# Two-layer cross-attention kernel: the context accumulated with its features on partitions

## The chip, the cores and the metric

The kernel runs on one core of a Trainium2 chip. The metric is the device time of one execution in microseconds (us), lower is better. Everything is one launch: a program for TensorE (PE in the profile), VectorE (DVE), ScalarE (ACT), GpSimd (POOL) and SyncE (SP), which keep step by semaphores alone.

## The reference

x and ctx are 8 sequences of 128 tokens with 128 features. Two layers follow each other, each an attention and a feed-forward part (FFN), all with residuals:

```python
x = x + xattn0(layernorm(x), ctx, ctx, mask, ...)   # 16 heads of 8, relative position bias, mask
x = x + ffn0(layernorm(x))                          # low rank: gelu((x U1) V1 + b1) U2 V2 + b2
x = x + xattn1(layernorm(x), ctx, ctx, ...)         # 16 heads of 8, no bias, no mask
x = x + moe(layernorm(x))                           # 16 experts of width 64, best 8, one shared expert
```

Either attention computes per head, with V = ctx Wv + bv:

```python
attn = softmax(energy)                # 128 queries x 128 keys
x = einsum('bhqk,bhkd->bhqd', attn, V)
x = concat(heads) @ Wo + bo
```

The softmax's division is put behind the product with V: the kernel multiplies unnormalized weights with V and with ones, and divides the one by the other. The part from there to `@ Wo` is called the context here.

## The kernel before

The 8 sequences are taken in 4 pairs (PAIRS); the two sequences of a pair are the batches b = 0, 1. A pass i of the loop body does layer 0 of pair i and, interleaved by hand, layer 1 of pair i - 1. The first pass (i = 0) has no layer 1, the last one (i = 3) doesn't start a new pair, and a tail behind it does layer 1 of the last pair. In the trace the first pass lies at about 27 to 69 us, the second to 130, the third to 191, the last to 252, the tail to 297. Each engine's order is written out in its own `body`, and an engine never goes past an instruction that waits.

PSUM has 8 banks of 128 x 512 fp32, in three rings: "m" (banks 4 to 6) for single results, "s" (0 and 1) for scores, "t" (2 and 3) for turned weights. BODY (L81) names the uses of a ring in order, and use n takes bank n modulo the ring's length: `fill` (L121) lets TensorE wait until the earlier use of that bank is freed, `filled` announces the result, `read` waits for it, `free` hangs on the reader's last instruction and gives the bank back, and `freed` waits for that. Of the "m" ring the text needs these. In the first pass the order is C00, xcT, C01, k0, k1, q0, o0 (L102), so k0 gets the bank of C00, q0 that of C01, and o0 that of k0. In the later passes it has C10, C11, o1, C00, C01, xn3T, logit, o0, so logit gets the bank of C00 and o0 that of C01.

The context of layer l and batch b:

- `values` (L1075, TensorE): the weights `pt` (keys on partitions, 128 queries per head slot) come in four chunks c of four slots s, each copied from PSUM by ScalarE. The stationary operand of a head is `va`, 128 keys x 32 columns (VW): 8 value features, a column of ones, and zeros. A matmul of slot s writes 32 partitions, at 32 j, and 128 columns of C, at 128 g; head = 8 (s % 2) + s // 2, j = head // 4, g = head % 4. So 16 matmuls fill a bank, with queries on columns. fp32 matmuls show as two records each.
- `context` (L758, VectorE): per batch a transpose of 32 x 32 blocks from PSUM to `ct1`, which frees the bank; the reciprocal of the row sums (`crc`, 16 columns); the multiply into `ct2`; and a second block transpose to `ct3`, features on partitions. Every kind is done for both batches before the next kind.
- `attention_out` (L1089, TensorE): waits for both `ct3` and multiplies with `wo` into o0 or o1. `add_residual` (L779), the variance, POOL's power (L375) and `normalize` (L721) follow.

TensorE's order around it: in the first pass values(0, 0), later values(0, 1), then keys(0) and keys(1) (L1015) and queries(0) (L1020) of the next pair, then attention_out(0). In the later passes values(1, 0), the turned scores of batch 1 (L1071), values(1, 1), half of the turned weights of layer 0 (L1060), attention_out(1), the other half, values(0, 0), values(0, 1), turn_tokens(3) (L999), logits (L1121), attention_out(0). The FFN of layer 0 has its matmuls at L1102 and L1113; L878 is VectorE's last addition before the output.

POOL does `add_value_bias` (L400; the operation is L406) once per layer and pair, one addition that writes the 8 value columns of all heads of both batches of `va`. In its order it stands, for layer 1, ahead of power(3) (the variance behind add_residual(1)). The splits of the next keys and queries (L394, L383, L398, L387) stand ahead of power(1) in the first pass. At the start VectorE clears `va` and sets its column of ones (L900, L902).

Of the kernel before, what the change touches and what calls it, by code (L numbers as in the profile page):

```python
# [11 lines left out]
ALU = mybir.AluOpType  # L12
AX = mybir.AxisListType

BATCH, SEQ, D = 8, 128, 128
# [23 lines left out]
VW = 32  # L39


def bass_xattn_ffn_moe(nc, x_d, ctx_d, mask_d, wqk_d, wv_d, wo_d, bqk_d, bv_d, rows_d, table_d, u1t_d, v1_d, b1_d,
# [3 lines left out]
    with ExitStack() as ctx:  # L46
# [166 lines left out]
        pt = sb("pt", [128, 2, 2, HEADS, SEQ])  # L213
        ct1 = sb("ct1", [128, 2, 4, 4, 32])
        crc = sb("crc", [128, 2, 4, 4])
        ct2 = sb("ct2", [128, 2, 4, 4, DK])
        ct3 = sb("ct3", [128, 2, 2, SEQ])
# [153 lines left out]
        def _(pool):  # L371
# [28 lines left out]
            def add_value_bias(l, p, turn):  # L400
                if l == 0:

                    freed(pool, "m", "v1", turn)
                elif not (isinstance(turn, int) and turn == 0):
                    read(pool, "m", "C11", turn)
                pool.tensor_tensor(va[:, l, :, :, 0:DK],  # L406
                                   vf[:].rearrange("p (b l h d) -> p b l h d", b=2, l=2, d=DK)[:, :, l],
                                   bvb[:].rearrange("p b (l h d) -> p b l h d", l=2, d=DK)[:, :, l],
                                   ALU.add).then_inc(sem(f"va{l}"), 1)

# [294 lines left out]
        def _(dve):  # L705
# [52 lines left out]
            def context(l, p, turn):  # L758

                for b in range(2):  # L760
                    src = read(dve, "m", f"C{l}{b}", turn)
                    free(dve.transpose(ct1[:, b], src[:]), "m", f"C{l}{b}", turn)  # L762
                for b in range(2):
                    freed(dve, "m", f"C{l}{b}", turn)
                    dve.reciprocal(crc[:, b], ct1[:, b, :, :, DK]).then_inc(sem(f"crc{l}"), 1)
                for b in range(2):
                    after(dve, f"crc{l}", p, b + 1, 2)
                    dve.tensor_tensor(ct2[:, b].rearrange("p q g d -> p g q d"), ct1[:, b, :, :, 0:DK],
                                      crc[:, b].unsqueeze(3).broadcast_to([128, 4, 4, DK]), ALU.mult)\
                       .then_inc(sem(f"ct2{l}"), 1)  # L770
                for b in range(2):
                    after(dve, f"ct2{l}", p, b + 1, 2)
                    dve.transpose(ct3[:, l, b], ct2[:, b]).then_inc(sem(f"ct3{l}"), 1)

# [125 lines left out]
            dve.memset(va[:], 0.0).then_inc(sem("va_zeros"), 1)  # L900
            dve.wait_ge(sem("va_zeros"), 1)
            dve.memset(va[:, :, :, :, DK:DK + 1], 1.0).then_inc(sem("va_cleared"), 1)  # L902
            dve.wait_ge(sem("ident_in"), 16)
# [89 lines left out]
        def _(pe):  # L993
# [81 lines left out]
            def values(l, b, p, turn):  # L1075

                if b == 0:
                    after(pe, f"va{l}", p)
                dst = fill(pe, "m", f"C{l}{b}", turn)
                for c in range(4):  # L1080
                    freed(pe, "t", f"T{l}{b}{c}", turn)
                    for s in range(4 * c, 4 * c + 4):
                        head = HALF * (s % 2) + s // 2
                        j, g = head // 4, head % 4
                        ins = pe.matmul(dst[32 * j:32 * j + VW, g * SEQ:(g + 1) * SEQ], va[:, l, b, head],  # L1085
                                        pt[:, l, b, s], start=True, stop=True)
                filled(ins, "m", f"C{l}{b}", turn)

            def attention_out(l, p, turn):  # L1089
                after(pe, f"ct3{l}", p, of=2)  # L1090
                dst = fill(pe, "m", f"o{l}", turn)
# [288 lines left out]
```

## Time and profile before

| | |
|---|---|
| time, median of 3 runs | 300.1 us (300.08, 300.1, 301.48) |
| span of the profiled execution | 296.9 us (its own full time is not given) |
| PE busy | 209.6 us, 71% |
| PE weight loads | 154.6 us, 52% |
| DVE busy | 198.1 us, 67% |
| ACT busy | 118.0 us, 40% |
| POOL busy | 83.7 us, 28% |
| chain that ended last, by engine | PE 33%, DVE 27%, issue 15%, POOL 7%, ACT 6%, DMA 5%, SP's queue 5% |

Busy times overlap between engines and say only how full each is. The chain follows back from the last instruction to what released each step; its shares tell where the end is set. Times in the rows are in us from the start of the span unless marked ns.

### The profile page before, as it was taken

What the parts mean: (1) busy time and instruction counts of PE and PEld (TensorE: products, weight loads), DVE (VectorE), ACT (ScalarE), POOL (GpSimd) and SP (SyncE); (2) the same over time, 40 slices, a digit from 0 to 9 for tenths busy, and PEclk for the clock granted to TensorE, in tenths of its full rate; (3) what the DMA queues carried; (4) which work ended last, traced back from release to release, by engine and by line L of the source; (5) the groups of instructions that cost most, each with busy time, mean ns of one, the idle gap of its engine ahead of it and who ended that gap; (6) DMA issues with size and microseconds to landing.
All of it is one profiled execution on the core that took longest, in us unless ns stands there. A gap on an engine that the chain in (4) does not pass through costs nothing.

```text
span 296.9 us, 4777 instructions
## 1 busy us (share of the span) xinstructions
PE 209.6 (71%) x1541; PEld 154.6 (52%) x1541; DVE 198.1 (67%) x561; ACT 118.0 (40%) x273; POOL 83.7 (28%) x110
## 2 busy tenths in 40 slices
PE   2723674555987868767887787777976979572996
PEld 1422553343655747535566565554765756251684
DVE  4656866246886786678876976678578764915673
ACT  2500664603587363305683452153552612061221
POOL 1402676134436131315281312150412011000000
PEclk9955699555599999995899999967799889779699
DMA  3553612102101220030002200200020002000000
GB/s 110 185 144 99 235 46 67 49 2 59 33 3 25 62 64 13 11 97 0 2 15 58 70 18 0 67 5 4 7 51 0 0 2 53 20 2 2 0 0 18
DMA packets 21895, 12.61 MB, mean 42 GB/s; under 512 B 2966, under 2 KB 20998, under 8 KB 21878
## 3 DMA queue, kind: packets, MB, share of 16 engines
q1 hardware_dynamic: 20790, 11.88, 14.7%
q10 hardware_dynamic: 1088, 0.52, 0.7%
q8 instruction: 9, 0.15, 0.2%
q14 instruction: 8, 0.07, 0.1%
HBM read 5.44 MB, written 0.54 MB: 20 GB/s over the span
## 4 chain that ended last, share of the span: by engine, by line
PE 33%; DVE 27%; issue 15%; POOL 7%; ACT 6%; DMA 5%; SPq 5%; DVEq 0%; POOLq 0%; ACTq 0%
PE bank L1130 5%; PE bank L1085 4%; PE bank L1150 4%; DVE mx L743 3%; DVE xn L721 3%; POOL rstd L375 3%; ACT pt L554 3%; PE bank L1071 3%; POOL es L416 2%; DVE ct L762 2%; SPq L258 2%; SPq L261 2%; PE bank L1102 2%; DVE es L733 2%; PE bank L1039 2%
## 5 line engine op out<-in xcount | busy, mean ns | idle before, releaser
L416 POOL TENSOR_TENSOR es<-es,mx 128x512 f32<-128x512 f32 x32 | 33.4, 1055 | 37.9 <-DVE mx L728 36.8
L542 ACT ACTIVATE es<-es 128x512 f32<-128x512 f32 x32 | 19.1, 625 | 33.9 <-POOL es L416 33.8
L1060 PE MATMUL bank<-ident,es 128*128 128x128 f32 x128 | 25.4, 346 | 9.9 <-ACT es L542 9.7
L375 POOL TENSOR_TENSOR rstd<-ve,half 128x2 f32<-128x2 f32 x16 | 11.2, 699 | 73.8 <-DVE ve L715 73.4
L593 ACT ACTIVATE gth<-bank 128x256 f32<-128x256 f32 (+1 forms) x36 | 13.2, 380 | 34.1 <-PE bank L1130 34.0
L733 DVE TENSOR_TENSOR es<-bank,biasq 128x512 f32<-128x512 f32 x32 | 21.2, 684 | 7.8 <-PE bank L1044 7.7
L1060 PEld LDWEIGHTS bank<-ident,es 128*128 128x128 f32 x128 | 19.0, 178 | 14.1 <-ACT es L542 13.7
L1130 PE MATMUL bank<-xnT,wg 128*128 128x256 f32 (+1 forms) x72 | 25.6, 439 | 0.6 <-DVE gb L858 0.4
L852 DVE SCALAR_TENSOR_TENSOR ga<-gth,bank 128x256 f32<-128x256 f32 (+1 forms) x36 | 15.0, 416 | 15.0 <-ACT gth L593 14.9
L1085 PE MATMUL bank<-pt,va 128*32 128x128 f32 x512 | 24.8, 290 | 0.0
L1130 PE MATMUL bank<-xnT,wu 128*128 128x256 f32 (+1 forms) x72 | 22.9, 403 | 0.0
L1150 PE MATMUL bank<-wd,hT 128*128 128x128 f32 x128 | 20.9, 287 | 2.9 <-DVE hT L872 2.8
L547 ACT ACTIVATE pt<-bank 128x512 f32<-128x512 f32 x32 | 18.3, 593 | 11.7 <-PE bank L1060 11.5
L743 DVE TENSOR_REDUCE mx<-bank 128x4 f32<-128x512 f32 x32 | 20.3, 684 | 3.5 <-PE bank L1039 3.2
L554 ACT ACTIVATE pt<-bank 128x512 f32<-128x512 f32 x32 | 17.4, 594 | 11.8 <-PE bank L1071 11.6
L762 DVE STREAM_TRANSPOSE ct<-bank 128x512 f32<-128x512 f32 x16 | 11.0, 705 | 16.3 <-PE bank L1085 16.2
L1085 PEld LDWEIGHTS bank<-pt,va 128*32 128x32 f32 x512 | 20.7, 116 | 2.2 <-issue 1.1
L1150 PEld LDWEIGHTS bank<-wd,hT 128*128 128x128 f32 x128 | 18.1, 193 | 6.6 <-DVE hT L872 5.3
L728 DVE TENSOR_REDUCE mx<-es 128x4 f32<-128x512 f32 x32 | 21.0, 676 | 0.0
L999 PE MATMUL bank<-ident,xn 128*128 128x128 f32 x24 | 6.0, 337 | 20.2 <-DVE xn L721 20.2
L721 DVE TENSOR_SCALAR xn<-x,mv,rstd 128x128 f32<-128x128 f32 x32 | 12.9, 444 | 9.6 <-POOL rstd L375 9.6
L1044 PE MATMUL bank<-kst,qst 96*128 96x128 bf16 x128 | 13.6, 254 | 6.2 <-DVE es L733 3.6
(132 smaller groups left out, 408.8 us busy)
## 6 DMA issues: line engine op xcount, KB each, us to landing
kst<-ksp SPq DMA_DIRECT2D x24, 64.0 KB, 2.6
qst<-qsp SPq DMA_DIRECT2D x48, 32.0 KB
kst<-ksp SPq DMA_DIRECT2D x48, 32.0 KB
qst<-qsp SPq DMA_DIRECT2D x24, 64.0 KB, 2.5
biasq<-rel_bias_scratch SPq DMA_DIRECT2D x2, 512.0 KB, 4.6
wg<-in_wg SPq DMA_DIRECT2D x1, 544.0 KB, 4.1
wu<-in_wu SPq DMA_DIRECT2D x1, 544.0 KB, 5.6
wd<-in_wd SPq DMA_DIRECT2D x1, 512.0 KB, 5.7
```

What stands on the lines that cost most here:

```text
L375: pool.tensor_tensor(rstd[:, n, :], ve[:, n, :], half[:, 0:2], ALU.pow).then_inc(sem(f"rstd{n}"), 1)
L416: pool.tensor_tensor(es[:, b, h], es[:, b, h], mx[:, 0, b, h].unsqueeze(2).broadcast_to([128, 4, SEQ]), ALU.subtract).then_inc(sem(f"less0 ...
L542: act.activation(es[:, b, h], es[:, b, h], ACT.Exp, scale=-1.0).then_inc(sem(f"p0{b}"), 1)
L554: free(act.activation(pt[:, 1, b, 4 * c:4 * c + 4, :], src[:], ACT.Exp), "t", f"T1{b}{c}", turn)
L721: dve.tensor_scalar(xn[n][:, b], src[:, b], mv[:, n, b, 0:1], rstd[:, n, b:b + 1], ALU.subtract, ALU.mult).then_inc(sem(f"xn{n}"), 1)
L728: dve.tensor_reduce(mx[:, 0, b, 4 * c:4 * c + 4], es[:, b, 4 * c:4 * c + 4], AX.X, ALU.min)\
L733: free(dve.tensor_tensor(es[:, b, 4 * c:4 * c + 4], src[:].rearrange("p (h k) -> p h k", h=4), biasq[:, 2 * c:2 * c + 2].rearrange("p a b ...
L743: free(dve.tensor_reduce(mx[:, 1, b, 4 * c:4 * c + 4], src[:].rearrange("p (h k) -> p h k", h=4), AX.X, ALU.max), "s", f"S1{b}{c}", turn)
L1060: ins = pe.transpose(dst[:, s * SEQ:(s + 1) * SEQ], es[:, b, 4 * c + s], ident[:])
L1085: ins = pe.matmul(dst[32 * j:32 * j + VW, g * SEQ:(g + 1) * SEQ], va[:, l, b, head], pt[:, l, b, s], start=True, stop=True)
L1130: ins = pe.matmul(dst[0:rows, k * TOK:(k + 1) * TOK], w[:, c * 128:c * 128 + rows], xnT[3][:], start=True, stop=True)
L1150: ins = pe.matmul(Y_BANK[:, b * D:(b + 1) * D], hT[0:rows, c % 2, b * SEQ:(b + 1) * SEQ], wd[:, c] if c < ECH else swd[:], start=(c == 0 a ...
```

## The change

`values` now uses a different place for each head. In chunk c the four slots go to the four strips of 32 partitions, and the four chunks accumulate in the same 128 columns: `va` holds a head's 8 value columns at column 8 c of its 32, the others are zero. A second set of four matmuls per chunk, with the stationary operand `vones` (ones in the 8 columns at 8 c), accumulates the row sums in the next 128 columns, so that each sum stands on the same 8 partitions as the features that it divides. 32 matmuls per bank in place of 16, and C comes out with features on partitions.

`context` has four operations in place of eight: per batch a reciprocal of 128 x 128 from PSUM, then per batch a multiply from PSUM into `ct3`, which now frees the bank. `attention_out` waits for the freed banks. POOL adds the value bias in four pieces. The rows of `wo` and the columns of `wv` and `bv` are put in another order on the host.

The diff, cut (the same reordering of `bv` is left out):

```diff
@@ -211,9 +211,8 @@
         pt = sb("pt", [128, 2, 2, HEADS, SEQ])
-        ct1 = sb("ct1", [128, 2, 4, 4, 32])
-        crc = sb("crc", [128, 2, 4, 4])
-        ct2 = sb("ct2", [128, 2, 4, 4, DK])
+        vones = sb("vones", [128, 4, VW])
+        crc = sb("crc", [128, 2, SEQ])
         ct3 = sb("ct3", [128, 2, 2, SEQ])
@@ -403,10 +402,12 @@
-                pool.tensor_tensor(va[:, l, :, :, 0:DK],
-                                   vf[:].rearrange("p (b l h d) -> p b l h d", b=2, l=2, d=DK)[:, :, l],
-                                   bvb[:].rearrange("p b (l h d) -> p b l h d", l=2, d=DK)[:, :, l],
-                                   ALU.add).then_inc(sem(f"va{l}"), 1)
+                for c in range(4):
+                    h = slice(4 * c, 4 * c + 4)
+                    ins = pool.tensor_tensor(va[:, l, :, h, DK * c:DK * c + DK],
+                                             vf[:].rearrange("p (b l h d) -> p b l h d", b=2, l=2, d=DK)[:, :, l, h],
+                                             bvb[:].rearrange("p b (l h d) -> p b l h d", l=2, d=DK)[:, :, l, h], ALU.add)
+                ins.then_inc(sem(f"va{l}"), 1)
@@ -759,18 +760,11 @@
                 for b in range(2):
                     src = read(dve, "m", f"C{l}{b}", turn)
-                    free(dve.transpose(ct1[:, b], src[:]), "m", f"C{l}{b}", turn)
-                for b in range(2):
-                    freed(dve, "m", f"C{l}{b}", turn)
-                    dve.reciprocal(crc[:, b], ct1[:, b, :, :, DK]).then_inc(sem(f"crc{l}"), 1)
-                for b in range(2):
+                    dve.reciprocal(crc[:, b], src[:, SEQ:2 * SEQ]).then_inc(sem(f"crc{l}"), 1)
+                for b in range(2):
+                    src = read(dve, "m", f"C{l}{b}", turn)
                     after(dve, f"crc{l}", p, b + 1, 2)
-                    dve.tensor_tensor(ct2[:, b].rearrange("p q g d -> p g q d"), ct1[:, b, :, :, 0:DK],
-                                      crc[:, b].unsqueeze(3).broadcast_to([128, 4, 4, DK]), ALU.mult)\
-                       .then_inc(sem(f"ct2{l}"), 1)
-                for b in range(2):
-                    after(dve, f"ct2{l}", p, b + 1, 2)
-                    dve.transpose(ct3[:, l, b], ct2[:, b]).then_inc(sem(f"ct3{l}"), 1)
+                    free(dve.tensor_tensor(ct3[:, l, b], src[:, 0:SEQ], crc[:, b], ALU.mult), "m", f"C{l}{b}", turn)
@@ -898,8 +892,11 @@
             dve.memset(va[:], 0.0).then_inc(sem("va_zeros"), 1)
-            dve.wait_ge(sem("va_zeros"), 1)
-            dve.memset(va[:, :, :, :, DK:DK + 1], 1.0).then_inc(sem("va_cleared"), 1)
+            dve.memset(vones[:], 0.0).then_inc(sem("va_zeros"), 1)
+            dve.wait_ge(sem("va_zeros"), 2)
+            for c in range(4):
+                ins = dve.memset(vones[:, c, DK * c:DK * c + DK], 1.0)
+            ins.then_inc(sem("va_cleared"), 1)
@@ -1079,15 +1076,17 @@
                 for c in range(4):
                     freed(pe, "t", f"T{l}{b}{c}", turn)
-                    for s in range(4 * c, 4 * c + 4):
-                        head = HALF * (s % 2) + s // 2
-                        j, g = head // 4, head % 4
-                        ins = pe.matmul(dst[32 * j:32 * j + VW, g * SEQ:(g + 1) * SEQ], va[:, l, b, head],
-                                        pt[:, l, b, s], start=True, stop=True)
+                    for s in range(4):
+                        pe.matmul(dst[VW * s:VW * s + VW, 0:SEQ], va[:, l, b, 4 * c + s], pt[:, l, b, 4 * c + s],
+                                  start=(c == 0), stop=(c == 3), skip_group_check=True)
+                    for s in range(4):
+                        ins = pe.matmul(dst[VW * s:VW * s + VW, SEQ:2 * SEQ], vones[:, c], pt[:, l, b, 4 * c + s],
+                                        start=False, stop=(c == 3), skip_group_check=True)
                 filled(ins, "m", f"C{l}{b}", turn)
...
             def attention_out(l, p, turn):
-                after(pe, f"ct3{l}", p, of=2)
+                for b in range(2):
+                    freed(pe, "m", f"C{l}{b}", turn)
...
+    by_slot = lambda w: w.reshape(w.shape[0], 2, HALF, DK).swapaxes(1, 2).reshape(w.shape)
+    by_row = lambda w: by_slot(w.T).T.reshape(4, 4, DK, D).swapaxes(0, 1).reshape(D, D)
...
-        "wv": _np.stack([a["L0_xattn_Wv"], wv1], 1),
-        "wo": _np.stack([a["L0_xattn_Wo"], a["L1_xattn_Wo"]], 1),
+        "wv": _np.stack([by_slot(a["L0_xattn_Wv"]), by_slot(wv1)], 1),
+        "wo": _np.stack([by_row(a["L0_xattn_Wo"]), by_row(a["L1_xattn_Wo"])], 1),
```

## Rows read from the trace of the kernel before

**Rows 1.** Chain of waits, start and first pass: start us, us, what

```profile
24.34 2.30 DMA qst<-qsp
...
43.44 1.50 PE bank L1085 x32
...
46.85 0.70 PE bank L1093 x4
...
49.62 0.71 POOL rstd L375
```

**Rows 2.** Chain of waits, third pass

```profile
152.64 1.50 PE bank L1085 x32
...
156.51 0.72 PE bank L1093 x4
...
162.53 0.73 PE bank L1093 x4
```

**Rows 3.** Chain of waits, last pass and tail

```profile
208.68 2.72 PE bank L1085 x32
...
266.56 1.50 PE bank L1085 x32
...
269.93 0.73 PE bank L1093 x4
```

**Rows 4.** Page, costliest groups: busy us, mean ns, idle before

```profile
L1085 PE MATMUL bank<-pt,va 128*32 128x128 f32 x512 | 24.8, 290 | 0.0
```

**Rows 5.** Two instants, L1085 on PE: slice, length, busy (records in flight), clock, DMA

```profile
37.30:37.31 0.01, 0.01 (x6) 1.00 0.00 0
...
37.64:37.65 0.01, 0.01 (x11) 1.00 0.00 0
```

**Rows 6.** Timeline, third pass, PE: start, us, instruction, idle before and releaser

```profile
158.02 2.49 PE L1085 MATMUL bank<-pt,va 128*32 128x128 f32 x64
...
160.44 0.44 PE L999 MATMUL bank<-ident,xn 128*128 128x128 f32 x2
...
161.35 0.62 PE L1121 MATMUL bank<-gateT,xnT 128*128 128x16 f32 x4 [0.47 <-ACT xnT L489]
```

**Rows 7.** Instructions of the tile ct on DVE: ns min/median/max, first and last start

```profile
L762 DVE STREAM_TRANSPOSE ct<-bank x16: 672/708/718, 41.1 to 268.1; 128x512 f32<-128x512 f32 x16
L765 DVE RECIPROCAL crc<-ct x16: 207/220/234, 45.6 to 268.9; 128x16 f32<-128x16 f32 x16
L768 DVE TENSOR_TENSOR ct<-ct,crc x16: 253/280/698, 45.9 to 269.2; 128x128 f32<-128x128 f32 x16
L773 DVE STREAM_TRANSPOSE ct<-ct x16: 261/284/305, 46.3 to 269.6; 128x128 f32<-128x128 f32 x16
```

**Rows 8.** The smallest reciprocal, and a 128-column operation out of PSUM, same columns

```profile
L831 DVE RECIPROCAL swr<-sws x4: 166/166/166, 106.7 to 277.8; 128x2 f32<-128x2 f32 x4
...
L878 DVE TENSOR_TENSOR xout<-bank,x x8: 281/286/292, 130.1 to 294.3; 128x128 f32<-128x128 f32 x8
```

**Rows 9.** Timeline, first pass, PE and POOL

```profile
44.84 1.13 PE L1015 MATMUL bank<-xcT_sb,wqk 128*128 128x256 f32 x4
...
45.82 0.67 PE L1020 MATMUL bank<-xcT_sb,wqk 128*128 128x256 f32 x2
...
48.84 0.67 POOL L387 TENSOR_TENSOR qsp<-qr,qsp 128x256 bf16<-128x256 f32 x1
```

**Rows 10.** Instructions of L406 on POOL: ns min/median/max, first and last start

```profile
L406 POOL TENSOR_TENSOR va<-vf,bvb x8: 713/728/1167, 23.5 to 215.1; 128x256 f32<-128x256 f32 x8
```

**Rows 11.** Chain, first pass's FFN, and timeline of the same matmuls in the third

```profile
52.99 3.80 PE bank L1102 x8
...
60.25 3.77 PE bank L1113 x16
...
68.56 1.23 PE bank L1020 x2
...
176.90 1.95 PE L1113 MATMUL bank<-w,fh 128*128 128x128 f32 x16
```

More of the change, by code:

```diff
@@ L1352 @@
                           _np.stack([by_dim(wq1), by_dim(wk1)], 1)], 1),
-        "wv": _np.stack([a["L0_xattn_Wv"], wv1], 1),
-        "wo": _np.stack([a["L0_xattn_Wo"], a["L1_xattn_Wo"]], 1),
+        "wv": _np.stack([by_slot(a["L0_xattn_Wv"]), by_slot(wv1)], 1),
+        "wo": _np.stack([by_row(a["L0_xattn_Wo"]), by_row(a["L1_xattn_Wo"])], 1),
         "bqk": _np.stack([by_dim(a[f"L{l}_xattn_b{c}"].reshape(D)) for l in range(2) for c in "qk"], 1),
-        "bv": _np.tile(_np.concatenate([a["L0_xattn_bv"], a["L1_xattn_bv"].reshape(D)]), (2, 1)),
+        "bv": _np.tile(_np.concatenate([by_slot(a["L0_xattn_bv"].reshape(1, D))[0],
+                                        by_slot(a["L1_xattn_bv"].reshape(1, D))[0]]), (2, 1)),
         "rows": _np.stack([_np.tile(a[n], (2, 1)) for n in ("L0_xattn_bo", "L0_ffn_b2", "L1_xattn_bo")]),
```

## The prediction

> **What bounds the kernel now.** I read the page first: no engine is busy all the time, so the end is set by a chain, and the chain of waits has to be read stretch by stretch. At the places that the diff touches it always has the same order: the value matmuls of the second batch, VectorE's context work, the output projection. In the first pass these are the rows at 43.44 (ends 44.94) and 46.85, and the POOL step at 49.62 follows from them [rows 1]. In the third pass they are 152.64 (ends 154.14) and 156.51 for layer 1, and layer 0's projection follows at 162.53 [rows 2]; the second pass has the same distances. The last pass has a value stage at half clock, and the tail has one more layer-1 stage [rows 3]. So there are eight contexts, layer 0 in four passes, layer 1 in three and the tail, and all eight are on the chain.
>
> **Part 1, TensorE: 16 more matmuls per batch.** One value stage is 16 fp32 matmuls, two records each, in 1.50 us [rows 1]; it becomes 64 records. It matters in which column strips they lie. Now the matmuls alternate between two strips (head 0 in strip 0, head 8 in strip 2) and after eight of them go to the other two. A record lasts 0.29 us on average [rows 4]. One instant inside such a stretch has 6 records in flight; one at the change-over, when four strips are in use, has 11 [rows 5]. So one starts every 0.048 us in the first case (32 of them make the 1.5 us) and every 0.026 in the second. The new order s = 0 to 3 visits all four strips in turn, so I take the second rate: 64 x 0.026 = 1.7, with the last one's end 1.9 us. The stage grows by 0.4. Both batches of layer 0 run back to back in 2.49 us [rows 6]; 128 x 0.026 and the end make 3.6, which is 1.1 more. The bounds: no growth (a gain is excluded, as each strip gets twice the records at the same length of one), and the mean rate of those 64 records, 0.039, for all: 2.5 for a stage and 5.1 for a pair.
>
> **Part 2, VectorE.** Removed per context: two transposes of 512 columns (0.71 each), two reciprocals of 16 (0.22), two multiplies (0.28) and two transposes of 128 (0.28) [rows 7], some 2.5 us as they overlap. Behind the last value matmul 1.9 us of it lie on the chain in the first pass (44.94 to 46.85) and 2.35 in the loop (154.14 to 156.51), where one multiply takes 0.698 instead of 0.253 [rows 1, 2, 7]: its inputs are both in SBUF and POOL's value addition runs then. Added: a reciprocal of 128x128 out of PSUM per batch, and a multiply of 128x128 with one input in PSUM. The multiply is the shape of L878, 0.286, of which about 0.21 shows behind another one [rows 8]. The wide reciprocal isn't in the trace. Its low end is L878 again, 0.29; its high end is eight of the narrow ones, 8 x 0.22 = 1.77. Between them: 2 columns take 0.166 and 16 take up to 0.234 [rows 7, 8], so 14 columns cost up to 0.068, and 112 further ones 0.54: 0.234 + 0.54 = 0.77. I take 0.77, because the slope is measured on this very instruction. The Trainium skill, "VectorE: DVE Perf Modes", in the part on why there are eight slices, says that reciprocal is an iterative divide with a repeat count of eight. If that is eight cycles of the page's 0.96 GHz for each column, 128 columns are an estimated 1.07 us beside the fixed part, some 0.45 more than I take, and the sum below would end at 306.3; but by that rule 14 columns would cost 0.117, so the trace rather speaks against it.
>
> The first batch's reciprocal runs while TensorE still makes the second batch. The new step behind the last value matmul is then one reciprocal 0.77, two multiplies 0.21 each, and 0.1 of hand-over: 1.3 us. That saves 0.6 in the first pass and in the tail, and 1.05 in the loop's layer 1, where no multiply with two SBUF inputs is left.
>
> **Part 3, banks are held longer.** This weighs most. The old code frees a context's bank with the first transpose, before the other batch is touched. The new code frees C00 with its multiply, and in VectorE's order that stands behind the reciprocal of the second batch. In the first pass the ring gives keys(0) the bank of C00. Before, keys(0) starts at 44.84, right behind the values [rows 9]. After, the second batch is complete at 44.94 + 0.4 = 45.34, its reciprocal at 46.11, the first multiply at 46.34, and keys(0) starts near 46.36, 1.5 late. Behind it in TensorE's order come keys(1), queries(0) and only then the projection, whose bank is the one of keys(0), which ScalarE must have read. The projection moves from 46.85 to about 47.95, and the 0.6 of part 2 is lost. POOL's power at 49.62 stands in order behind the last split of the new query, at 48.84 [rows 1, 9], which comes 1.5 late too: 50.36 + 0.67 = 51.03. **First pass: +1.4.**
>
> **Layer 1 in passes 2 and 3.** Two value stages, one of them ahead of the other batch's scores and exponentials, both on the chain: +0.8; part 2: -1.05. The projection comes 0.25 earlier.
>
> **Layer 0 in passes 2 and 3.** The values start at 158.02 - 0.25 and are complete 3.6 later, at 161.4 instead of 160.5. Reciprocal and first multiply: 162.4. The logits take the bank of C00 and stand ahead of the projection in TensorE's order; they start at 161.35 before [rows 6], at 162.4 after, and with 0.45 of issue the projection is at 162.85 instead of 162.53 [rows 2]. **+0.3 each.**
>
> **Last pass.** Its first layer-1 value stage took 2.72 at half clock [rows 3], which is 0.9 more instead of 0.4 if the level stays, and the context behind layer 1 saves only 0.6, as in the first pass: +1.3. With full clock it is about +0.3. The level hangs on what came before, so I take the middle, **+0.8**. **Tail:** one value stage on the chain (the other lies beside a DMA): 0.4 - 0.6 = **-0.2** on a context that now ends at 269.93 [rows 3].
>
> **Edits costed at nothing.** POOL adds the value bias in four pieces of 64 columns; one of 256 takes 0.73 [rows 10], four take between 0.73 and 2.9, and I take 1.5. In the loop POOL's next work waits for VectorE's variance, over 2.5 us behind; if that cover went, up to 2 us per pass would show. The setup's one larger and three small extra memsets lie beside the stack DMA that the first scores wait for [rows 1]. The reordered weights cost no device time, and no DMA changes its size.
>
> **Sum.** 1.4 + 0.3 + 0.3 + 0.8 - 0.2 = 2.6. The profiled execution has a span of 296.9; its own full time isn't given, and the three timed runs lie 3.2 above that span with their median 300.1. I keep that distance: span 299.5, time **302.7**.
>
> **Rivals.**
> - *The wide reciprocal costs what a multiply costs*, 0.29. For it: transposes of 512 and of 128 columns differ by 1.1 ns a column [rows 7]. Against: the two narrow reciprocals. It takes 0.48 from each step; in the loop's layer 0 the logits then wait for the turned tokens instead. First pass +0.9, passes 2 and 3 -0.3 each, last +0.1, tail -0.7: 299.8. Chance 0.15.
> - *The other side: TensorE's clock in the first pass.* Matmuls at 52.99 and 60.25 ran at half clock, 3.80 and 3.77, and L1020 at 68.56 took 1.23; the second kind takes 1.95 at full clock later, so such stages halve [rows 11]. TensorE now does more just before, and all of it moves by over 1 us, so the rise from 1.2 to 2.4 GHz may come here instead of a pass later. From the point where it comes ahead of the first of these stages it gives back 1.8 + 1.8 + 0.6 = 4.2: 298.5, faster. Behind the first it gives 2.4: 300.3. Against: TensorE still waits often there. Chance 0.12.
> - *Issue binds.* The four-strip rate holds only for queued records: 0.7 more for a single stage, 1.5 for a pair, so 0.7 + 3 x 2.9 + 0.7, about 10: 313. The row of 11 in flight speaks against it, though it shows one instant. Chance 0.10.
> - *The wide reciprocal is dear.* Its cost per column stays near that of a whole narrow instruction: half way to the bound, 1.27, it adds 0.5 to each of eight contexts, 306.7; at the bound 310.7. Chance 0.15.
> - That the change doesn't do what it says can be left out: the transposes are gone from the code.
>
> **Numbers.** The forecast (0.48) has its own range, 301 to 304.5, for the clock of the last pass. Half a per cent, 1.5 us, is about what a measurement here can tell from no change: faster is below 298.6, slower above 301.6. Faster: 0.08 of the clock case and 0.02 of the cheap reciprocal, 0.10. Same: 0.13, 0.04 and the lower edge of the forecast, 0.07, make 0.24. Slower: 0.66. The range 298.9 to 309 leaves out the best clock case (0.08), the issue case (0.10) and the dearest reciprocal (0.02).
>
> **What would show it.** Values: 64 records in 1.9 us, a pair in 3.6. A RECIPROCAL of 128x128 near 0.77. In the first pass L1015 waiting for the first multiply, and the projection near 48. The logits waiting for VectorE instead of ScalarE. A record every 0.04 us, a reciprocal under 0.4 or over 1.1, or an FFN stage of the first pass in 2 us instead of 3.8 would make the sum wrong.

## The result, and the profile after

The changed kernel takes **304.17 us** (median of 17 runs, 301.67 to 307.97) where the kernel before, run beside it on the same chip, takes 301.22 (17 runs, 298.85 to 302.77). The ratio is **1.0086, interval 1.0055 to 1.0118**; the forecast of 302.7 over 300.1 was 1.0087. The ratio leaves out the changed kernel's four slow runs (306.24 to 307.97); the medians of all runs are 2.95 us apart, 0.98%. The profiled span is 302.4 (296.9 before), the mean granted clock 0.853 (0.839 before).

The page's groups for the new work (line, engine, operation, output and input, count | busy us, mean ns | idle before and releaser):

```profile
L763 DVE RECIPROCAL crc<-bank 128x128 f32<-128x128 f32 x16 | 15.3, 955 | 22.1 <-PE bank L1083 22.1
L1080 PE MATMUL bank<-pt,va 128*32 128x128 f32 x512 | 28.3, 296 | 0.0
L1083 PE MATMUL bank<-pt,vones 128*32 128x128 f32 x512 | 27.8, 292 | 0.0
```

One record of a value matmul takes what it took [rows 4]; there are twice as many. The reciprocal takes 955 ns, where I had taken 770.

The timeline of the first pass (start, us, engine and instruction, idle before and releaser):

```profile
43.29 0.42 PE L1080 MATMUL bank<-pt,va 128*32 128x128 f32 x8
...
44.85 0.40 PE L1083 MATMUL bank<-pt,vones 128*32 128x128 f32 x8
45.31 0.96 DVE L763 RECIPROCAL crc<-bank 128x128 f32<-128x128 f32 x1 [3.36 <-PE bank L1083]
46.19 0.23 DVE L767 TENSOR_TENSOR ct<-bank,crc 128x128 f32<-128x128 f32 x1
46.56 1.10 PE L1012 MATMUL bank<-xcT_sb,wqk 128*128 128x256 f32 x4 [1.32 <-DVE ct L767]
...
48.26 0.68 PE L1092 MATMUL bank<-wo,ct 128*128 128x128 f32 x4 [0.16 <-ACT kf L515]
...
51.17 0.70 POOL L374 TENSOR_TENSOR rstd<-ve,half 128x2 f32<-128x2 f32 x1
```

The values start where they started [rows 1] and are complete at 45.25. Keys(0), L1012, wait 1.32 us for the first batch's multiply, where before they followed the values at once [rows 9]. The projection comes at 48.26 (was 46.85) and POOL's power at 51.17 (was 49.62) [rows 1].

The third pass, same columns; the first three lines belong to layer 1, the others to layer 0:

```profile
158.26 1.16 POOL L407 TENSOR_TENSOR va<-vf,bvb 128x64 f32<-128x64 f32 x4
159.09 0.48 DVE L767 TENSOR_TENSOR ct<-bank,crc 128x128 f32<-128x128 f32 x2
159.67 0.68 PE L1092 MATMUL bank<-wo,ct 128*128 128x128 f32 x4 [0.50 <-DVE ct L767]
...
161.96 0.70 POOL L374 TENSOR_TENSOR rstd<-ve,half 128x2 f32<-128x2 f32 x1 [2.55 <-DVE ve L716]
...
164.92 0.96 DVE L763 RECIPROCAL crc<-bank 128x128 f32<-128x128 f32 x1 [0.75 <-PE bank L1083]
165.79 0.42 DVE L767 TENSOR_TENSOR ct<-bank,crc 128x128 f32<-128x128 f32 x2
...
166.17 0.59 PE L1120 MATMUL bank<-gateT,xnT 128*128 128x16 f32 x4 [0.95 <-DVE ct L767]
166.61 0.69 PE L1092 MATMUL bank<-wo,ct 128*128 128x128 f32 x4
```

Three things are to be seen. The two multiplies take 0.48 together though POOL's value addition (158.26 to 159.42) runs beside the first and most of the second: with an input in PSUM they aren't stretched, as the old ones were [rows 7]. The logits, L1120, now wait for VectorE; before, their releaser was ScalarE [rows 6]. And POOL's next work after the value addition waits 2.55 us for VectorE, so the addition's 1.16 in four pieces costs nothing.

Where the time came from, in starts of the eight output projections (first matmul of each, from the two timelines) and the ends of the spans:

| | 1st pass | 2nd, l1 | 2nd, l0 | 3rd, l1 | 3rd, l0 | last, l1 | last, l0 | tail | end |
|---|---|---|---|---|---|---|---|---|---|
| before | 46.85 | 95.63 | 101.64 | 156.51 | 162.53 | 216.88 | 222.90 | 269.93 | 296.9 |
| after | 48.26 | 97.39 | 104.33 | 159.67 | 166.61 | 223.31 | 230.25 | 275.29 | 302.4 |
| shift | 1.41 | 1.76 | 2.69 | 3.16 | 4.08 | 6.43 | 7.35 | 5.36 | 5.5 |

Each step from layer 1 to layer 0 within a pass costs 0.92 more, 6.94 instead of 6.02, three times alike. The jump of 2.35 ahead of the last pass and the 2 us given back behind it are in good part the clock: an FFN stage of the third pass takes 2.74 instead of 1.99 and the last pass's first value stage 3.52 instead of 2.79, while an FFN stage of the last pass takes 1.99 instead of 2.89.

### The profile page after: what moved, and what is told of

Its sections match the earlier page's. It is cut to its first block, busy times and chain, and to the rows that moved or that the text cites. A ratio compares the mean times of both kernels' runs of the same rounds, so it can differ in the third digit from the quotient of the medians.

```text
span 302.4 us, 5812 instructions
## 1 busy us (share of the span) xinstructions
PE 218.1 (72%) x2053; PEld 163.4 (54%) x2053; DVE 195.5 (65%) x533; ACT 117.9 (39%) x273; POOL 87.5 (29%) x134
## 4 chain that ended last, share of the span: by engine, by line
PE 37%; DVE 21%; issue 18%; POOL 9%; ACT 8%; SPq 4%; DMA 3%; DVEq 0%; POOLq 0%; ACTq 0%
PE bank L1080 6%; PE bank L1129 5%; PE bank L1083 5%; DVE mx L744 4%; PE bank L1149 4%; POOL es L417 4%; DVE xn L722 3%; PE bank L1068 3%; POOL rstd L374 2%; ACT pt L555 2%; SPq L260 2%; DVE es L734 2%; DVE mx L729 2%; PE bank L1057 2%; PE bank L1112 2%
## 5 line engine op out<-in xcount | busy, mean ns | idle before, releaser
L763 DVE RECIPROCAL crc<-bank 128x128 f32<-128x128 f32 x16 | 15.3, 955 | 22.1 <-PE bank L1083 22.1
L1080 PE MATMUL bank<-pt,va 128*32 128x128 f32 x512 | 28.3, 296 | 0.0
L1083 PE MATMUL bank<-pt,vones 128*32 128x128 f32 x512 | 27.8, 292 | 0.0
L1129 PE MATMUL bank<-xnT,wg 128*128 128x256 f32 (+1 forms) x72 | 26.4, 453 | 0.5 <-DVE gb L852 0.4
L1129 PE MATMUL bank<-xnT,wu 128*128 128x256 f32 (+1 forms) x72 | 23.6, 412 | 0.0
L1041 PE MATMUL bank<-kst,qst 96*128 96x128 bf16 x128 | 14.6, 268 | 4.7 <-DVE es L734 2.6
```

The lines of the kernel that those rows point to most:

```text
L1080: pe.matmul(dst[VW * s:VW * s + VW, 0:SEQ], va[:, l, b, 4 * c + s], pt[:, l, b, 4 * c + s], start=(c == 0), stop=(c == 3), skip_group_chec ...
L1083: ins = pe.matmul(dst[VW * s:VW * s + VW, SEQ:2 * SEQ], vones[:, c], pt[:, l, b, 4 * c + s], start=False, stop=(c == 3), skip_group_check= ...
L1129: ins = pe.matmul(dst[0:rows, k * TOK:(k + 1) * TOK], w[:, c * 128:c * 128 + rows], xnT[3][:], start=True, stop=True)
```

## The experiments

All ratios are to the kernel before, run beside on the same chip, and 1% is 3 us. Code lines that a cut leaves out are marked by `...`.

**The reciprocal by itself.** The kernel before with a sweep of widths at the start of VectorE's work, each instruction waiting for the one ahead of it, so that none overlaps.

```diff
...
+            for src in (rsrc, rsrc, Y_BANK):
+                for w in (2, 16, 32, 64, 128, 256, 512):
+                    dve.reciprocal(rdst[:, 0:w], src[:, 0:w]).then_inc(sem("rsw"), 1)
+                    n += 1
+                    dve.wait_ge(sem("rsw"), n)
```

> The kernel before with a row of reciprocals at VectorE's start, each waited for: 2, 16, 32, 64, 128, 256 and 512 columns, twice out of SBUF and once out of PSUM. The time of the whole means nothing here. Three lines are possible for 128 columns and the slope: 0.77 us and 4.8 ns a column (my forecast's slope from the two narrow ones), 0.96 us and about 6.3 ns a column (what L763 of the changed kernel shows if its fixed part is that of the narrow one), 1.2 us and 8.3 ns a column (eight cycles each). I now expect the second, and PSUM and SBUF alike.

The groups of this line by form (columns as on the page; the source is an SBUF tile or a PSUM bank):

```profile
L893 DVE RECIPROCAL gb<-bank 128x512 f32<-128x512 f32 x1 | 3.4, 3357 | 0.0
L893 DVE RECIPROCAL gb<-gb 128x128 f32<-128x128 f32 x2 | 1.9, 953 | 0.1
L893 DVE RECIPROCAL gb<-bank 128x128 f32<-128x128 f32 x1 | 1.0, 957 | 0.0
L893 DVE RECIPROCAL gb<-gb 128x16 f32<-128x16 f32 x2 | 0.5, 253 | 0.1
L893 DVE RECIPROCAL gb<-gb 128x2 f32<-128x2 f32 x2 | 0.3, 166 | 0.1
```

From 128 to 512 columns it is (3357 - 957) / 384 = 6.25 ns for each column, from 16 to 128 it is (953 - 253) / 112 = 6.25 again, and about 0.15 us is fixed. PSUM costs 4 ns more than SBUF. The forecast's slope (4.9 ns, 0.068 us over 14 columns) was too low because of its 16-column point: by itself that form takes 253 ns, not the 207 to 234 of [rows 7]. In the kernel before both batches' narrow reciprocals overlap the instruction ahead of them (two take 0.36 together at 45.59); where each waits, as in the better order below, one takes 0.25. The Trainium skill, "VectorE: DVE Perf Modes", section "First, the fixed hardware budget", names a repeat count of eight for reciprocal. At that page's 0.96 GHz eight cycles are an estimated 8.3 ns; the trace doesn't agree, the measured column is six of them.

**The reciprocal taken out of the changed kernel.** A copy stands in its place, so the division is left out.

```diff
-                    dve.reciprocal(crc[:, b], src[:, SEQ:2 * SEQ]).then_inc(sem(f"crc{l}"), 1)
+                    dve.tensor_copy(crc[:, b], src[:, SEQ:2 * SEQ]).then_inc(sem(f"crc{l}"), 1)
```

> The changed kernel with a copy of 128x128 from PSUM in place of each reciprocal; the division is left out (the context is multiplied by its row sums). Theory (the reciprocal's 0.958 us is paid once in each of the eight contexts on the chain): copy near 0.28, 0.67 less per context, five to six us in all: ratio to the kernel before 0.988 to 0.994. Rival (the second batch's reciprocal hides behind other waits): under 2 us, ratio over 1.0.

298.91 us (10 runs), ratio 0.9967 (0.9936 to 0.9998), span 296.7. Its timeline in the first pass, and the logits of the third:

```profile
44.65 0.29 DVE L763 COPY crc<-bank 128x128 f32<-128x128 f32 x1 [4.03 <-PE bank L1083]
44.86 0.28 DVE L767 TENSOR_TENSOR ct<-bank,crc 128x128 f32<-128x128 f32 x1
45.28 1.10 PE L1012 MATMUL bank<-xcT_sb,wqk 128*128 128x256 f32 x4 [0.70 <-DVE ct L767]
...
46.98 0.68 PE L1092 MATMUL bank<-wo,ct 128*128 128x128 f32 x4 [0.16 <-ACT kf L515]
...
162.17 0.62 PE L1120 MATMUL bank<-gateT,xnT 128*128 128x16 f32 x4 [0.47 <-ACT xnT L490]
```

Keys(0) still wait, 0.70 instead of 1.32. If one reciprocal's excess were paid in each of eight contexts, it would be 8 x (0.958 - 0.292) = 5.3 us. The profile shows less. From the start of the second value stage to the projection it is 0.62 less in the first pass (4.35 for 4.97) and 0.66 in each of the four layer-1 contexts (2.82 for 3.48), but the step from layer 1 to layer 0 shrinks by only 0.29 (6.65 for 6.94), three times, because the logits then wait for ScalarE's turned tokens, as in the kernel before. Together that is 4.1 us. The ratio falls by 0.0119 against the result above and by 0.0194 against the third pair below, 3.6 to 5.8 us. The expected 0.988 to 0.994 was missed on the small side. With a copy in that place the changed scheme is as fast as the kernel before or slightly faster: the loss is no more than what the wide reciprocal costs above a copy. That doesn't make the reciprocal the only cause, as the next variant shows.

**The row-sum matmuls taken out.** The division is then by a wrong number (the context itself); the row sums aren't computed.

```diff
-                    dve.reciprocal(crc[:, b], src[:, SEQ:2 * SEQ]).then_inc(sem(f"crc{l}"), 1)
+                    dve.reciprocal(crc[:, b], src[:, 0:SEQ]).then_inc(sem(f"crc{l}"), 1)
...
-                    for s in range(4):
-                        ins = pe.matmul(dst[VW * s:VW * s + VW, SEQ:2 * SEQ], vones[:, c], pt[:, l, b, 4 * c + s],
-                                        start=False, stop=(c == 3), skip_group_check=True)
```

> The changed kernel without the 16 matmuls per batch that make the row sums; the reciprocal reads the context itself, so the division is by the wrong number and the row sums are left out. Matmul count per stage is that of the kernel before, but over four strips. Theory (four strips, one record per 0.027 us): a stage is 32 records in about 1.05 us, shorter than the 1.5 of the kernel before, a pair 1.95; gain against the changed kernel about 0.85 per single stage and 1.75 per pair, some 11 us over all if TensorE's stages are wholly on the chain: ratio to the kernel before 0.965 to 0.98. Rival (stages are bound by what ScalarE delivers): stages shorten but the projection moves by less than half of it, ratio 0.99 to 1.0.

295.78 us (5 runs), ratio 0.9853 (0.9807 to 0.9900), the largest gain of all variants, with the reciprocal still in, and between the 0.965 to 0.98 expected and the rival's 0.99. The profiled execution took 300.06, so its span isn't used. The timeline of the third pass, PE:

```profile
151.58 1.94 PE L1080 MATMUL bank<-pt,va 128*32 128x128 f32 x32
...
155.56 1.20 PE L1080 MATMUL bank<-pt,va 128*32 128x128 f32 x32
...
160.03 1.95 PE L1080 MATMUL bank<-pt,va 128*32 128x128 f32 x64
...
163.88 0.59 PE L1117 MATMUL bank<-gateT,xnT 128*128 128x16 f32 x4 [1.40 <-DVE ct L767]
```

The pair of layer 0 takes 1.95 instead of 3.70. Only half of these 1.75 us reaches the end: layer 0's projection follows layer 1's by 6.04 instead of 6.94, since the logits then wait 1.40 for VectorE, whose two reciprocals (1.76) have become the limit. A single stage takes 1.08 to 1.20 where the clock is full, but 1.94 where it isn't, as at 151.58, and most single stages of this profile are of that kind (mean granted clock 0.794). So this profile shows the price at the pair alone, and the ratio (2.3 points under the result) mixes it with the clock.

**Two strips at a time instead of four**, with the same 32 matmuls per context and batch.

```diff
...
+                    for pair in ((0, 1), (2, 3)):
+                        for s in pair:
+                            pe.matmul(dst[VW * s:VW * s + VW, 0:SEQ], va[:, l, b, 4 * c + s], ...)
+                        for s in pair:
+                            ins = pe.matmul(dst[VW * s:VW * s + VW, SEQ:2 * SEQ], vones[:, c], ...)
```

> The changed kernel with the same 32 matmuls per batch in another order: slots 0 and 1 with their row sums, then slots 2 and 3, so at most two strips alternate. Theory (the strips run beside each other and a strip needs 0.109 us per record): 64 records in 2.6 to 3.5 us per stage instead of 1.9, a pair 5 to 7; 0.7 to 1.6 more per single stage, eight single and three pair stages: ratio to the kernel before 1.03 to 1.06. Rival (the rate is set by issue, order is of no matter): 1.9 us per stage, ratio as the changed kernel's, 1.009.

A stage takes 1.98 us instead of 1.95, a pair 3.72 instead of 3.70. An instant inside a stage, first of the changed kernel, then of this one (window, length, PE busy and records in flight, other engines, clock, DMA share, GB/s):

```profile
43.90:43.91 0.01, 0.01 (x12) 0.01 (x4) 0.00 (x0) 0.01 (x2) 0.00 (x0) 1.00 0.42 102
```

```profile
43.90:43.91 0.01, 0.01 (x10) 0.01 (x2) 0.00 (x0) 0.00 (x0) 0.00 (x0) 1.00 0.00 0
```

Ten records in flight where I looked for about six. Matmuls of the next pair evidently start while this pair's strips still work, so switching every four matmuls keeps nearly all four busy. What differs in the old kernel is the run length, eight matmuls in the same two strips; run length by itself was not varied. The 2.6 us or more expected for a stage fell. The measured time, 306.33 (4 runs), ratio 1.0236 (1.0185 to 1.0286), is higher than the stages explain; that stays open. Its interval overlaps those of the two later measurements of the changed kernel below.

**The four strips in the kernel before** (transposes and narrow reciprocals kept): slot s goes to strip s, value and output weights are reordered to suit.

```diff
-                        head = HALF * (s % 2) + s // 2
-                        j, g = head // 4, head % 4
-                        ins = pe.matmul(dst[32 * j:32 * j + VW, g * SEQ:(g + 1) * SEQ], va[:, l, b, head],
+                        j, g = s % 4, c
+                        ins = pe.matmul(dst[32 * j:32 * j + VW, g * SEQ:(g + 1) * SEQ], va[:, l, b, s],
...
```

> The kernel before, its transposes and its 16 matmuls per batch kept, with slot s of a chunk in strip s and the chunk as the column block, so that consecutive matmuls visit all four strips (weights reordered on the host as in the change). Theory: 32 records in 1.05 to 1.1 us instead of 1.5, a pair in 1.95 instead of 2.49; 0.4 less on each single stage on the chain and 0.5 on each pair, 4 to 5 us in all: ratio 0.982 to 0.99. Rival (the old order already overlaps all that it can, or the chunk's arrival bounds it): 0.996 to 1.0.

299.79 us (12 runs), ratio 1.0005 (0.9968 to 1.0042). The stages shrink as expected, 1.54 to 1.08 and 2.49 to 1.95 for the pair, and nothing comes of it; the expected 0.982 to 0.99 was wrong. The second pass, layer 1, and two lines of the third:

```profile
91.77 1.19 PE L1084 MATMUL bank<-pt,va 128*32 128x128 f32 x32
...
93.02 0.72 DVE L762 STREAM_TRANSPOSE ct<-bank 128x512 f32<-128x512 f32 x1 [0.59 <-PE bank L1084]
...
93.94 1.53 DVE L768 TENSOR_TENSOR ct<-ct,crc 128x128 f32<-128x128 f32 x2
...
94.55 0.78 POOL L406 TENSOR_TENSOR va<-vf,bvb 128x256 f32<-128x256 f32 x1
...
96.02 0.71 PE L1092 MATMUL bank<-wo,ct 128*128 128x128 f32 x4 [1.80 <-DVE ct L773]
...
152.60 1.18 PE L1084 MATMUL bank<-pt,va 128*32 128x128 f32 x32
...
155.84 0.71 PE L1092 MATMUL bank<-wo,ct 128*128 128x128 f32 x4 [0.79 <-DVE ct L773]
```

The same multiplies in the kernel before:

```profile
94.18 0.90 DVE L768 TENSOR_TENSOR ct<-ct,crc 128x128 f32<-128x128 f32 x2
```

In the second pass the earlier end moved both multiplies, whose inputs are both in SBUF, under POOL's three operations from 93.29 to 95.33: 1.53 for the two, 0.90 before. The projection comes 4.25 behind the stage's start, 3.96 before. That is not so in every pass: in the third it comes 3.24 behind it instead of 3.94, in the last 3.12 instead of 3.44. In layer 0 the pair ends 0.5 earlier, but VectorE's normalization, ahead of the context in its order, ends only about when the transposes start, at 99.59, and the step from layer 1 to layer 0 stays 6.01. And five single stages run at half clock (1.92 to 1.94), two before; the mean clock is 0.811. Two of the five are the second stages of the first pass and of the tail, where the projection comes 3.90 and 3.86 behind the stage's start instead of 3.48 and 3.44. So over these five contexts gains of 1.0 stand against losses of 1.1, most of the losses at half clock. Whether the shorter stages bring the lower clock about was not tested.

**The bank held longer, in the kernel before.** Only the release moves, from the first transpose to the multiply; no work is added.

```diff
-                    free(dve.transpose(ct1[:, b], src[:]), "m", f"C{l}{b}", turn)
+                    dve.transpose(ct1[:, b], src[:]).then_inc(sem(f"ct1{l}"), 1)
@@
+                    free(dve.tensor_tensor(ct2[:, b].rearrange("p q g d -> p g q d"), ...), "m", f"C{l}{b}", turn)
```

> The kernel before with one thing moved: the bank of a context is freed by its multiply (third kind of operation) and no longer by its first transpose. No operation is added. Theory (the release order costs by itself): keys(0) of the first pass start near 46.2 instead of 44.84, the first projection near 47.8 instead of 46.85, POOL's power about 1.2 later; in the later passes the logits start about 0.7 later and the layer-0 projection 0 to 0.3 later. Sum 1.2 to 2 us, ratio 1.004 to 1.007. Rival (other work covers it): ratio 0.998 to 1.002.

301.17 us (12 runs), ratio 1.0057 (1.0020 to 1.0094). The first pass:

```profile
42.72 1.54 PE L1085 MATMUL bank<-pt,va 128*32 128x128 f32 x32
...
45.23 0.46 DVE L768 TENSOR_TENSOR ct<-ct,crc 128x128 f32<-128x128 f32 x2
...
45.63 1.10 PE L1015 MATMUL bank<-xcT_sb,wqk 128*128 128x256 f32 x4 [1.37 <-DVE ct L768]
...
47.32 0.68 PE L1093 MATMUL bank<-wo,ct 128*128 128x128 f32 x4 [0.16 <-ACT kf L514]
```

The wait of the changed kernel appears without its other parts: 1.37 ahead of keys(0), and the projection stands 4.60 behind the start of the values, 3.49 before. That is +1.1, and POOL's power comes 7.51 behind that start instead of 6.26. The third pass keeps its distances (3.95 and 6.01), so this part is paid once. The expected 1.004 to 1.007 is met.

**The bank released early, in the changed kernel.** VectorE inverts and divides batch 0 before it touches batch 1.

```diff
                     dve.reciprocal(crc[:, b], src[:, SEQ:2 * SEQ]).then_inc(sem(f"crc{l}"), 1)
-                for b in range(2):
-                    src = read(dve, "m", f"C{l}{b}", turn)
                     after(dve, f"crc{l}", p, b + 1, 2)
```

> The changed kernel with VectorE's order per batch: reciprocal and multiply of the first batch, then those of the second; C00 is freed before C01 is even complete. My theory (the late release of the bank is the largest term of the first pass): L1012 of the first pass starts right behind the values, near 45.25 instead of 46.56, the first projection near 46.9 instead of 48.26, the logits wait for ScalarE again, and the multiply of the first batch leaves the end of the chain (0.2 per context). Time 0.990 to 0.995 of the changed kernel, so 0.999 to 1.004 of the kernel before. Rival (the bank is a detail and the reciprocal is the whole loss): under 1 us gained, ratio to the kernel before 1.005 or more.

302.14 us (9 runs), ratio 1.0080 (1.0047 to 1.0113), where 0.999 to 1.004 was expected. In the first pass, with the logits of the third:

```profile
46.41 1.13 PE L1010 MATMUL bank<-xcT_sb,wqk 128*128 128x256 f32 x4
46.55 0.96 DVE L763 RECIPROCAL crc<-bank 128x128 f32<-128x128 f32 x1 [4.65 <-PE bank L1081]
...
47.54 0.29 DVE L765 TENSOR_TENSOR ct<-bank,crc 128x128 f32<-128x128 f32 x1
...
47.98 0.67 PE L1015 MATMUL bank<-xcT_sb,wqk 128*128 128x256 f32 x2 [0.45 <-DVE ct L765]
...
166.42 0.62 PE L1118 MATMUL bank<-gateT,xnT 128*128 128x16 f32 x4 [0.47 <-ACT xnT L490]
```

Keys(0) follow the values with no wait, and the logits wait for ScalarE again. The queries wait 0.45 for the second batch instead. But the value stage ahead took 3.10, at half clock, so that this profile's projection (48.49) is no earlier, and one pair of ratios from two chips (1.0080 and 1.0086) tells nothing. So I ran the changed kernel once more, and then both on one chip.

> The changed kernel once more, on the same chip as the two variants of the kernel before, as the measure for them: 1.009 of the kernel before, between 1.004 and 1.014. The profile tells how far TensorE's granted clock differs from the first profile of the same kernel: if the 5.5 us between the two profiled spans was mostly clock, this span lies nearer to 300 than to 302.

303.42 us (6 runs), ratio 1.0148 (1.0085 to 1.0211), just above the expected range, span 299.9.

> The changed kernel with the early release once more, now beside the changed kernel itself on the same chip. Its first profile had TensorE at half clock during the first pass's second value stage (3.10 us instead of 1.95), which hid what the release does. With full clock there: keys near 45.2, first projection near 46.9. Ratio 0.002 to 0.007 below the changed kernel's.

> The changed kernel, as the measure for the early release on the same chip: 1.007 to 1.014 of the kernel before. A third profile of it: the reciprocal 0.958, the stages 1.95 and 3.70 at full clock, with half-clock stretches elsewhere than in the first two.

On one chip the early release gives 302.02 (12 runs), ratio 1.0075 (1.0040 to 1.0111), and the changed kernel 305.63 (6 runs), ratio 1.0161 (1.0113 to 1.0209). The intervals just don't overlap: holding the bank costs some 0.9% here, about 2.6 us. The size isn't firm, since the changed kernel's own ratios are 1.0086, 1.0148 and 1.0161, and the early order's two (1.0080 and 1.0075) lie close to the first of them. The profiles show 1.8 of it: in the first pass the projection comes 2.0 behind the end of the last value matmul (46.47 to 48.49) instead of 3.0 (45.25 to 48.26), and in the loop layer 0's projection follows layer 1's by 6.68 instead of 6.94, three times, since the logits' bank too is free earlier. In the second profile of the early order, too, the first pass's second value stage ran at half clock (3.26).

**A better order in the kernel before.** In layer 1 and in the first pass VectorE does all four steps of batch 0, then those of batch 1; layer 0 in the loop stays interleaved.

```diff
...
+                steps = (turned, inverted, divided, back)
+                if l == 1 or (isinstance(turn, int) and turn == 0):
+                    order = [(f, b) for b in range(2) for f in steps]
+                else:
+                    order = [(f, b) for f in steps for b in range(2)]
```

> The kernel before with VectorE's order changed alone: in layer 1 and in the first pass the first batch gets all four steps (transpose, reciprocal, multiply, transpose) before the second is touched; TensorE's order, matmuls and layouts are those of the kernel before. Theory (what lies behind the last value matmul decides, and the first batch's part fits into the wait for the second): 1.9 and 2.35 us shrink to about 1.55, so 0.4 in the first pass and the tail and 0.4 to 0.8 in each layer-1 context: 2 to 3 us, ratio 0.990 to 0.994. Rival (each step waits for its own predecessor, which the interleaving hid, or the multiply again meets POOL's addition): 0.998 to 1.004.

**297.56 us (9 runs), ratio 0.9913 (0.9877 to 0.9948)**: it beats both kernels, by 2 to 3 us as expected. The second pass, DVE:

```profile
88.93 0.72 DVE L762 STREAM_TRANSPOSE ct<-bank 128x512 f32<-128x512 f32 x1
89.68 0.25 DVE L766 RECIPROCAL crc<-ct 128x16 f32<-128x16 f32 x1
89.97 0.61 DVE L770 TENSOR_TENSOR ct<-ct,crc 128x128 f32<-128x128 f32 x1
90.61 0.31 DVE L776 STREAM_TRANSPOSE ct<-ct 128x128 f32<-128x128 f32 x1
92.30 0.72 DVE L762 STREAM_TRANSPOSE ct<-bank 128x512 f32<-128x512 f32 x1 [1.38 <-PE bank L1096]
...
93.34 0.29 DVE L770 TENSOR_TENSOR ct<-ct,crc 128x128 f32<-128x128 f32 x1
```

Batch 0 is done, its stretched multiply (0.61) too, in time in which VectorE waited anyway. Behind the values of batch 1 lie four single steps. The projection starts 3.39 behind the start of those values, 3.96 before; in the third pass it is 3.73 instead of 3.94, in the last 3.32 instead of 3.44, in the first 3.37 instead of 3.49. Together these are 1.0 of the 2.6 us that the ratio says; the rest isn't located (mean clock 0.879 in this profile, 0.839 in that of before). The clock is a rival for it. At a mean clock of 0.844 or 0.845 two runs of this order averaged 298.1, five of the kernel before 298.8; at 0.827 to 0.829 three averaged 298.5, six of the kernel before 300.3; and the kernel before's two runs at 0.873 took 297.68 and 297.85. At equal clock the gain is thus 0.7 to 1.8, from few runs. What is shown of the order itself is the 1.0 us that is located.

**The same with four strips**, to see whether the shorter stages pay once VectorE's part is shorter.

> The same with the four-strip order of the matmuls from the variant of the kernel before. The four-strip order alone gave nothing. If that was because layer 0's pair waits for VectorE and the layer-1 stage only brought the multiply under POOL's additions, it gives at most 0.4 per single stage here: ratio 0.985 to 0.993, 0 to 0.005 below the variant without it. Rival (a shorter stage lets TensorE's clock fall more often and gives nothing): equal to it within 0.002.

298.44 us (12 runs), ratio 0.9955 (0.9915 to 0.9994), outside the expected 0.985 to 0.993. In its second pass both multiplies take 0.73, under POOL's work, and the projection starts 4.18 behind the values' start, against 3.39 without the strips. In the third it is 3.05 against 3.73, but six single stages of this profile run at half clock. The strips don't help here either.

## Why the prediction was right, point by point

**Value stages.** The step took 1.9 for a single stage and 3.6 for a pair, from one record every 0.026 us. Measured: 1.95 and 3.70, 0.027 a record. Right, and the bound of 2.5 and 5.1 with the "issue binds" rival fell: an instant shows 12 records in flight.

**The wide reciprocal** is the mis-sized term: 0.77 taken, 0.958 measured. The slope came from two narrow widths, one of which was overlapped. The dear-reciprocal rival started at 1.27, so neither that nor the cheap one (0.29) holds. The price lies between the forecast and the estimate made with the Trainium skill's "VectorE: DVE Perf Modes" (1.07 and the fixed part), and the forecast's remark that the trace speaks against that estimate rested on the overlapped reciprocals.

**First pass.** Forecast: keys(0) 46.36, projection 47.95, power 51.03. Measured: 46.56, 48.26, 51.17. They come 0.20, 0.31 and 0.14 later than forecast, about the reciprocal's 0.19, and the mechanism is shown by itself in the kernel before (+1.1 and +1.25).

**Layer 1 in passes 2 and 3.** Forecast -0.25. In the third pass, from the start of values(1,0) to the projection, it is 7.27 instead of 7.32: -0.05, the reciprocal's 0.19 again.

**Layer 0 in passes 2 and 3.** The forecast puts it 0.57 later relative to layer 1's projection. Measured 0.92 (6.94 for 6.02). 0.19 is the reciprocal and 0.1 the longer pair, the other 0.06 isn't located; the logits wait 0.95 for VectorE as the forecast said. So a pass costs +0.87, not +0.3.

**Last pass and tail.** The half-clock value stage is there (3.52), 0.73 more than the 2.79 of before, where the forecast's middle stood for 0.4 or 0.9. The two cases of that middle don't match: +1.3 counts a saving of 0.6 behind layer 1, +0.3 one of 1.05, as in the passes ahead. With 0.6 in both they are 1.3 and 0.8, so the middle would be 1.05 and the whole forecast 302.95. The tail's last value stage takes 1.96 and the projection comes 3.47 behind its start, 3.44 before: no gain instead of -0.2.

**The sum.** With the measured terms, 1.55 + 0.87 + 0.87, the last pass at some 0.87 and 0.3 for its clock, and 0 for the tail make about 4.5 us instead of 2.6. The two later measurements of the changed kernel, 1.0148 and 1.0161, are 4.4 and 4.8 us; the first, 1.0086 (1.7 to 3.5 us), does not fit, and 2.95 us between the medians of all those runs doesn't quite either. So the agreement of the first ratio with the forecast to four digits is partly luck; the direction and the places are shown. A pair of profiles can't price the change: the changed kernel's three spans, 302.4, 299.9 and 301.2, lie 5.5, 3.0 and 4.3 above the 296.9. And 296.9 is itself a low value. The runs here whose span and time are both known take 1.8 to 2.1 us more than their span, which makes it about 298.7, 2.5 under the median that was measured beside the result.

**The clock rival.** The first pass's FFN stages stay near half clock, 3.48 and 3.42, where they took 3.80 and 3.77 [rows 11], although TensorE does more ahead of them. It didn't happen; both are some 0.3 shorter than before, no more. **POOL and the setup** cost nothing, as forecast: 1.16 in four pieces under 2.55 of waiting, and the first scores' input lands at 26.57 (26.64 before).

## What to carry to other kernels

Replacing eight small instructions of a context by four, two of them wide, pays only if the wide one's price per column is known: sweep it with a wait between the instructions, since records that overlap their predecessor give too low a slope. When a step now reads a buffer later, count what the late release holds up, by the reading engine's own order; one reordered loop won back about half of a loss here and, in the old kernel, 0.9%, of which 1.0 us is located. A shorter TensorE stage is worth nothing by itself if the next engine isn't free, if its work slides under another's use of the same memory, or if the stage then runs at half clock.

## What the runs showed of the hardware

- Reciprocal on VectorE: 6.25 ns for each fp32 column and 0.15 us fixed, 4 ns more out of PSUM, where a copy of 128 columns takes 0.292 in all.
- 32-column strips: four together give a 128-column fp32 record every 0.027 us, two, in runs of eight matmuls, give one every 0.048; alternating pairs of strips every four matmuls is as good as all four in turn (1.98 against 1.95).
- A multiply with one input in PSUM keeps its 0.23 to 0.29 beside POOL; with both in SBUF it takes up to 0.81.
- Half-clock stretches sit elsewhere in each profile of one and the same kernel: the first value stage of the second pass took 3.17 in one profile of the changed kernel and 1.95 or 1.96 in the two others, and both profiles of the early order had one at the first pass's second value stage, where all three of the changed kernel had full clock. Gains of a few tenths of a microsecond per stage can't be read off two spans; distances within a pass at equal clock can.
